# Attention denominators: ten blocks added by GpSimd, six by one DMA chain, two counted sums, reciprocals taken in place in PSUM

## The reference, cut to what matters

```
q = _heads(x @ Wq, B, L, nh, hd)                       # 16 heads of 32
decay_bias = -abs(pos[None, :] - pos[:, None]) * (1.0 - decay_factor)
out_short = _attention(q, k_s, v_s, decay_bias)        # softmax(q k^T / sqrt(hd) + bias) v
out_long  = _attention(q, k_l, v_l, None)
alpha = sigmoid(mix_weight)
out = alpha * out_short + (1.0 - alpha) * out_long     # then @ Wo
```

## Time and profile before

| | |
|---|---|
| median of 3 runs | 5075.12 us (5067.31 to 5075.18) |
| profiled execution | 5071.46 us |
| its span, first to last instruction | 5069.4 us |
| TensorE busy over the span | 4808.1 us (95%) |
| VectorE busy | 4044.8 us (80%) |
| GpSimd busy | 3012.3 us (59%) |
| ScalarE busy | 2998.2 us (59%) |

### The profile page before, as it was taken

The page is one execution under the profiler, slowest core; times in us unless marked ns, Lnnn a source line. Parts: engine busy times, 40 slices in busy tenths (PEclk is TensorE's granted clock), DMA queues, the critical chain, the costliest instruction groups (busy, mean ns, idle before and its releaser), DMA issues. The chain is left out here.

```text
span 5069.4 us, 101554 instructions
## 1 busy us (share of the span) xinstructions
PE 4808.1 (95%) x31276; PEld 2103.4 (41%) x31276; DVE 4044.8 (80%) x6613; ACT 2998.2 (59%) x5234; POOL 3012.3 (59%) x1267
## 2 busy tenths in 40 slices
PE   6888799999999999999999999999999599999998
PEld 3443233333333333333333333333332377777776
DVE  5556688888888888888888888888886388888887
ACT  2222166777676777777777777776767355555554
POOL 0000067878788888888887878888888233333332
PEclk9999789999999999999999999999999699999999
DMA  4332356777677776767676767777666200000000
GB/s 144 117 117 87 108 128 168 170 176 170 173 166 177 169 173 167 174 170 172 168 170 173 171 172 167 175 171 172 166 164 152 85 24 26 26 26 26 20 28 11
DMA packets 216978, 661.83 MB, mean 131 GB/s; under 512 B 38099, under 2 KB 111955, under 8 KB 158997
## 3 DMA queue, kind: packets, MB, share of 16 engines
q0 software_dynamic: 64512, 469.79, 39.8%
q1 hardware_dynamic: 151957, 185.66, 12.2%
HBM read 123.56 MB, written 61.64 MB: 37 GB/s over the span
## 5 line engine op out<-in xcount | busy, mean ns | idle before, releaser
L852 DVE TENSOR_REDUCE rowmax_parts<-scores_qk 128x1 f32<-128x512 f32 x4096 | 2524.6, 679 | 463.7 <-PE scores_qk L925 463.7
L832 ACT ACTIVATE probs_T<-scores_kq 128x512 f32<-128x512 f32 x4096 | 2286.3, 596 | 979.3 <-PE scores_kq L925 915.8
L766 POOL TENSOR_TENSOR probs_added<-probs_added,probs_T 128x2048 f32<-128x2048 f32 x448 | 2030.1, 4531 | 459.2 <-ACT probs_T L832 447.8
L925 PE MATMUL scores_kq<-q_operand,k_operand 103*128 103x512 f16 (+3 forms) x3712 | 1274.7, 349 | 10.2 <-ACT probs_T L832 8.3
L925 PE MATMUL scores_qk<-k_operand,q_operand 96*128 96x512 f16 (+4 forms) x3712 | 1123.1, 352 | 43.2 <-DMA k_operand<-positions_dram 19.4
L996 PE MATMUL outputs_T<-probs_T,v_operand 128*32 128x512 f32 x8192 | 1091.9, 605 | 1.3 <-ACT probs_T L832 1.3
L925 PEld LDWEIGHTS scores_kq<-q_operand,k_operand 103*128 103x128 f16 x3712 | 358.7, 97 | 920.9 <-ACT probs_T L832 635.7
L925 PEld LDWEIGHTS scores_qk<-k_operand,q_operand 96*128 96x128 f16 (+1 forms) x3712 | 354.8, 98 | 438.3 <-DVE rowmax_parts L852 184.4
L1602 PE MATMUL f_gate_up<-w_gate_up,xq_T 128*128 128x256 f16 (+1 forms) x4608 | 494.1, 265 | 8.6 <-DVE hidden L1493 7.5
L1602 PEld LDWEIGHTS f_gate_up<-w_gate_up,xq_T 128*128 128x128 f16 x4608 | 421.2, 98 | 77.8 <-issue 25.4
L766 POOL TENSOR_TENSOR probs_added<-probs_T 128x2048 f32<-128x2048 f32 x64 | 290.2, 4535 | 238.4 <-ACT probs_T L832 238.4
(11 more groups left out here) (165 smaller groups left out, 4302.1 us busy)
## 6 DMA issues: line engine op xcount, KB each, us to landing
probs_poured<-probs_T POOLq DMA_DIRECT2D x448, 1024.0 KB, 7.2
qk_parts_dram<-qk_parts SPq DMA_DIRECT2D x96, 256.0 KB, 2.5
q_operand<-qk_parts_dram SPq DMA_DIRECT2D x192, 128.0 KB, 2.6
k_operand<-qk_parts_dram SPq DMA_DIRECT2D x192, 128.0 KB, 3.1
v_dram<-v_heads SPq DMA_DIRECT2D x16, 1024.0 KB, 5.7
v_operand<-v_dram SPq DMA_DIRECT2D x64, 256.0 KB, 6.3
q_operand_above<-qk_parts_dram SPq DMA_DIRECT2D x96, 128.0 KB, 2.8
x_groups<-x SPq DMA_DIRECT2D x8, 1024.0 KB, 9.6
```

The source lines that it names most:

```text
L766: nc.gpsimd.tensor_tensor(total, first, probs[:, b % PBUF, :], ALU.add).then_inc(added.sem, 1)
L832: nc.scalar.activation(probs[:, kb % PBUF, qt * BANK:(qt + 1) * BANK], pb[:, k % 2, :], ACT.Exp)\
L852: nc.vector.reduce_max(rowmax[:, w % 2, c // NQ, c % NQ:c % NQ + 1], pa[:, k % 3, :], AX.X)\
L925: return nc.tensor.matmul(out, lhsT, rhs, start=start, stop=stop, skip_group_check=True)
```

## The change

The sixteen blocks of a unit are shared out anew. GpSimd adds ten (1, 2, 4, 5, 7, 8, 10, 11, 13, 14: nine add instructions where there were eight), and one DMA chain takes six (0, 3, 6, 9, 12, 15) in place of two chains with seven. The chain's tile is doubled, one for even and one for odd units. TensorE counts two tiles in place of three: GpSimd's in step 1 of the next unit and the chain's in step 4. ScalarE's copy of `sums` is gone: VectorE takes the reciprocals in place in PSUM, and `weigh`, now in step 9, reads them from there. The addition of the two kinds moves from VectorE to GpSimd's list, ahead of the add of block 11 in every second unit, and `weigh` of the next pair waits for it.

```diff
-WEIGH = 10
+WEIGH = 9
 MIX = 11
-BY_POOL = (0, 1, 3, 5, 7, 9, 11, 13, 14)
-BY_DMA = ((2, 6, 10), (4, 8, 12, 15))
+BY_DMA = (0, 3, 6, 9, 12, 15)
+BY_POOL = tuple(b for b in range(KB) if b not in BY_DMA)
-COUNT_POURED = (14, KB + 3)
 COUNT_ADDED = KB + 1
-TAKE_SUMS = 5
+COUNT_POURED = KB + 4
...
-            def pour(w, n, b, c):
+            def pour(w, n, b):
+                i = BY_DMA.index(b)
+                total, landed = poured_sum[:, w % 2, :], poured[w % 2]
                 wait_apart(pool, expd, expd.at(n, (w * KB + b + 1) * NQ), passed)
                 if i == 0:
+                    wait_apart(pool, counted_poured, counted_poured.at(n, w - 1), passed)
+                    nc.gpsimd.dma_start(total, probs[:, b % PBUF, :]).then_inc(landed.sem, 16)
                 else:
+                    wait_apart(pool, landed, landed.at(n, w // 2 * POURS + i), passed)
+                    nc.gpsimd.dma_start(total, probs[:, b % PBUF, :], accum_op=ALU.add).then_inc(landed.sem, 16)
+            def mix(p, n):
+                wait_apart(pool, weighed, weighed.at(n, 2 * p + 2), passed)
+                wait_apart(pool, stored[p], stored[p].before(n, NQ), passed)
+                nc.gpsimd.tensor_tensor(o_mix[:, p, :], o_w[:, 0, :], o_w[:, 1, :], ALU.add).then_inc(mixed.sem, 1)
...
-            def take_sums(w, n):
-                act.wait_ge(counted_poured[1].sem, counted_poured[1].at(n, w + 1))
-                act.wait_ge(weighed.sem, weighed.at(n, w))
-                nc.scalar.copy(sums[:, :], pc[:, :]).then_inc(sums_out.sem, 1)
...
             def invert(w, n, r):
-                dve.wait_ge(sums_out.sem, sums_out.at(n, w + 1))
-                nc.vector.reciprocal(inv[:, r * P:(r + 1) * P], sums[:, r * P:(r + 1) * P]).then_inc(inverted.sem, 1)
+                dve.wait_ge(counted_poured.sem, counted_poured.at(n, w + 1))
+                nc.vector.reciprocal(pc[:, r * P:(r + 1) * P], pc[:, r * P:(r + 1) * P]).then_inc(inverted.sem, 1)
...
-                nc.vector.scalar_tensor_tensor(o_w[:, w % 2, :], oT[:, w % 2, :], gates[:, 3 + w % 2:4 + w % 2], inv[:, :],
+                if w == 2:
+                    dve.wait_ge(mixed.sem, mixed.at(n, 1))
+                elif w == 0 and (not isinstance(n, int) or n > 0):
+                    dve.wait_ge(mixed.sem, mixed.before(n, 2))
+                nc.vector.scalar_tensor_tensor(o_w[:, w % 2, :], oT[:, w % 2, :], gates[:, 3 + w % 2:4 + w % 2], pc[:, :],
...
             def count_added(w, n):
+                pe.wait_ge(weighed.sem, weighed.at(n, w))
                 pe.wait_ge(added.sem, added.at(n, (w + 1) * ADDS))
-                count(added_sum[:, w % 2, :], counted, False, False)
+                count(added_sum[:, w % 2, :], counted, True, False)
+            def count_poured(w, n):
+                landed = poured[w % 2]
+                pe.wait_ge(landed.sem, landed.at(n, (w // 2 + 1) * POURS))
+                count(poured_sum[:, w % 2, :], counted_poured, False, True)
```

More of the change, by code:

```diff
@@ L574 @@
 INVERT = 5
-WEIGH = 10
+WEIGH = 9
 MIX = 11
-BY_POOL = (0, 1, 3, 5, 7, 9, 11, 13, 14)
-BY_DMA = ((2, 6, 10), (4, 8, 12, 15))
+BY_DMA = (0, 3, 6, 9, 12, 15)
+BY_POOL = tuple(b for b in range(KB) if b not in BY_DMA)
 ADDS = len(BY_POOL) - 1
-POURS = [len(blocks) for blocks in BY_DMA]
-COUNT_POURED = (14, KB + 3)
+POURS = len(BY_DMA)
 COUNT_ADDED = KB + 1
-TAKE_SUMS = 5
+COUNT_POURED = KB + 4
 def adds_until(kb):
@@ L619, in attend @@
         added_sum = sb("probs_added", [P, 2, L], F32)
-        poured_sum = [sb(f"probs_poured{i}", [P, L], F32) for i in range(2)]
+        poured_sum = sb("probs_poured", [P, 2, L], F32)
         rowmax = sb("rowmax_parts", [P, 2, KB, NQ], F32)
@@ L625, in attend @@
         oT = sb("o_T", [P, 2, BANK], F32)
-        sums = sb("sums_T", [P, BANK], F32)
-        inv = sb("sums_inverse", [P, BANK], F32)
         o_w = sb("o_weighed", [P, 2, BANK], F32)
@@ L652, in attend @@
         added = Rises(sem("a_added"), UNITS * ADDS, credit=1)
-        poured = [Rises(sem(f"a_poured{i}"), UNITS * POURS[i], 16) for i in range(2)]
+        poured = [Rises(sem(f"a_poured{i}"), UNITS // 2 * POURS, 16) for i in range(2)]
         counted = Rises(sem("a_counted"), UNITS, credit=1)
-        counted_poured = [Rises(sem(f"a_counted_poured{i}"), UNITS, credit=1) for i in range(2)]
+        counted_poured = Rises(sem("a_counted_poured"), UNITS, credit=1)
         taken = Rises(sem("a_o_taken"), UNITS, credit=1)
-        sums_out = Rises(sem("a_sums_out"), UNITS, credit=1)
         inverted = Rises(sem("a_inverted"), UNITS * NQ)
@@ L746, in _ @@
         def _(pool):
-            give_credit(pool, [maxed, expd, summed, added, counted, taken, sums_out, weighed] + counted_poured + stored)
+            give_credit(pool, [maxed, expd, summed, added, counted, taken, weighed, counted_poured] + stored)
             nc.gpsimd.memset(ones[:, :], 1.0).then_inc(consts, 1)
@@ L759, in add @@
                 wait_apart(pool, expd, expd.at(n, (w * KB + b + 1) * NQ), passed)
-                if b == 1:
-                    first = probs[:, 0, :]
+                if b == BY_POOL[1]:
+                    first = probs[:, BY_POOL[0], :]
                     wait_apart(pool, counted, counted.at(n, w - 1), passed)
@@ L766, in add @@
                 nc.gpsimd.tensor_tensor(total, first, probs[:, b % PBUF, :], ALU.add).then_inc(added.sem, 1)
-            def pour(w, n, b, c):
-                i = BY_DMA[c].index(b)
+            def pour(w, n, b):
+                i = BY_DMA.index(b)
+                total, landed = poured_sum[:, w % 2, :], poured[w % 2]
                 wait_apart(pool, expd, expd.at(n, (w * KB + b + 1) * NQ), passed)
                 if i == 0:
-                    wait_apart(pool, counted_poured[c], counted_poured[c].at(n, w), passed)
-                    nc.gpsimd.dma_start(poured_sum[c][:, :], probs[:, b % PBUF, :]).then_inc(poured[c].sem, 16)
-                else:
-                    wait_apart(pool, poured[c], poured[c].at(n, w * POURS[c] + i), passed)
-                    nc.gpsimd.dma_start(poured_sum[c][:, :], probs[:, b % PBUF, :], accum_op=ALU.add)\
-                        .then_inc(poured[c].sem, 16)
@@ L780, in one_pass @@
-            def one_pass(n):
-                for w in range(UNITS):
-                    for b in range(1, KB):
-                        if b in BY_POOL:
-                            add(w, n, b)
[L785 to L790, removed]
+                    wait_apart(pool, counted_poured, counted_poured.at(n, w - 1), passed)
@@ new lines, in one_pass @@
+            def one_pass(n, first, last):
+                for w in range(UNITS):
+                    back = unit_before(w, n, first)
+                    for b in range(KB):
+                        if b == MIX and back and back[0] % 2:
+                            mix(back[0] // 2, back[1])
+                        if b in BY_DMA:
+                            pour(w, n, b)
+                        elif b != BY_POOL[0]:
+                            add(w, n, b)
+            one_pass(0, True, False)
@@ L792, in _ @@
+            with nc.Fori(0, (PASSES - 2) // TURN, engines=[pool.engine], hint_back_edge=True) as m:
+                for i in range(TURN):
+                    one_pass(m * TURN + (i + 1), False, False)
+            one_pass(PASSES - 1, False, True)
+            mix(1, PASSES - 1)
         @block.scalar
@@ L812, in one_pass @@
                 for w in range(UNITS):
-                    back = unit_before(w, n, first)
                     for kb in range(KB):
-                        if back and kb == TAKE_SUMS:
-                            take_sums(*back)
                         if kb == (TURN_MAX + 2) % KB and after(w, n, last):
@@ L826, in one_pass @@
                         elif u >= 0 or not first:
-                            c = int(b in BY_DMA[1])
-                            act.wait_ge(poured[c].sem, poured[c].at(n, u * POURS[c] + BY_DMA[c].index(b) + 1))
+                            landed = poured[u % 2]
+                            act.wait_ge(landed.sem, landed.at(n, u // 2 * POURS + BY_DMA.index(b) + 1))
                         for qt in range(NQ):
@@ L839, in _ @@
             one_pass(PASSES - 1, False, True)
-            take_sums(UNITS - 1, PASSES - 1)
         @block.vector
@@ L904, in one_pass @@
                                 negate(*unit)
-                        if back and i == MIX and back[0] % 2:
-                            mix(back[0] // 2, back[1])
             one_pass(0, True, False)
@@ L912, in _ @@
             one_pass(PASSES - 1, False, True)
-            end = (UNITS - 1, PASSES - 1)
             for r in range(NQ):
-                invert(*end, r)
-            weigh(*end)
-            mix(1, PASSES - 1)
+                invert(UNITS - 1, PASSES - 1, r)
+            weigh(UNITS - 1, PASSES - 1)
         @block.tensor
@@ L1005, in count @@
                 mm.then_inc(done.sem, 1)
[L1007 to L1012, removed]
```

(9 more changed lines are left out.)

## The result

The changed kernel takes 5135.0 us (median of 4 runs, 5120.63 to 5141.65) against 5071.2 for the kernel before (5066.52 to 5075.18): a ratio of 1.0122, 95% interval 1.0098 to 1.0147. It is slower by about 62 us by that ratio (64 by the two medians), where 38 less had been forecast. The profiled execution took 5134.4 us, with a span of 5132.3.

What follows compares the result with a forecast made beforehand. The loop of exp, TensorE's product with v, count and next score was taken to set the pace; from 5071.5 us, -55 - 6 + 0 + 16 + 5 gave 5031.5, say 5033 us; range 5005 to 5110.

Steps and rivals of the forecast that it cites:

- Three counts become two: TensorE's counts in each unit: one count less saves 0.86 us in each of 64 units, -55.0 us.
- The weighing at step 9: `weigh` moved into VectorE's gap of 0.52 us: 0.1 us a unit, -6 us; bounds 0 and -20 us.
- Reciprocals in PSUM: VectorE's reciprocals written to PSUM: taken as 0; bounds -16 us and 40 us.
- Weighing beside GpSimd's adds: `weigh` on VectorE, reading one operand from PSUM, is not held while GpSimd adds: 0.
- GpSimd's list: GpSimd's work of 42.1 us, 0.1 for the semaphore and L turn in 50.7 us a unit: +16 us.
- L: Landing of block 0's pour, counted from its issue on GpSimd's queue: taken as 8.5 us, 11.2 beside loads.
- Some overlap is likely: Block 0's pour partly overlaps block 15's accumulating one, whose engines are not full all the time; L taken as 8.5.
- the undisturbed case: Block 0's data go behind the accumulating pour's, without loads beside: 6.9 + 2.7 - 0.9 = 8.7 us.
- the first rival: GpSimd becomes the bound: each us of L above 8.3 adds 63 us; slower, chance 0.20.
- its deciding point at 9.1: The L from which GpSimd's list turns in 51.3 us a unit and nothing is won.
- Other waits: Block 15's pour some 3 us later, its count one step later: just covered; exp's ring of eight blocks suffices.
- The end: Last unit: GpSimd falls 5 us further behind the last exp; the copy goes, the addition takes its time: +5 us.

Runs made afterwards that it cites:

- the first experiment: The kernel before with one count of its first DMA chain left out (blocks 2, 6 and 10 missing from the sums): 5016.7 us, ratio 0.9896.
- the second: The changed kernel with block 15's pour left out (the block missing from the sums): 5008.3 us, ratio 0.9876 to the kernel before.
- the last two experiments: Changed kernel with block 0's pour issued ahead of block 15's, plus the mixing back on VectorE: 5105.7 us; or plus reciprocals written to SBUF: 5360.9 us.
- the third experiment: The changed kernel with the loads of the next pass's operands issued six steps later: 5095.0 us, ratio 1.0043 to the kernel before.

## Why the prediction was wrong, point by point

- **Three counts become two**: right; 53 us measured, 55 said.
- **The weighing at step 9**: within its bounds. A unit with two counts takes 50.58 us with the weighing at step 10 (the first experiment) and 50.42 at step 9 (the second), 0.16 less; 0.1 had been taken. The two kernels differ in more than this step, so it is not a price of the step alone.
- **Reciprocals in PSUM**: nearly free, as taken. The row that answers to L874 of before has a median of 957 ns against 942:

```profile
L872 DVE RECIPROCAL sums<-sums x220: 953/957/960, 940.0 to 3779.3; 128x128 f32<-128x128 f32 x110
```

- **Weighing beside GpSimd's adds**: right. In the changed kernel `weigh` takes 734 to 742 ns, and the one of 2050.68 us ran beside an add that began at 2050.32 and took 4.53. The rule of the Trainium skill (GPSIMD Engine Reference, "1. Specifications"), that VectorE instructions with two SBUF inputs contend with GpSimd, is borne out by the last two experiments (2.7 and 4.15 us).
- **GpSimd's list**: well sized in the sum: 42.1 us and 0.1 for the semaphore said, 41.8 and 0.6 measured in the mean of 55 units. The semaphore's part was put too low by 0.5, the work too high by 0.3. A pour takes 0.91 us of the list (2013.76 to 2019.38, less an add of 4.71), 0.95 said; the moved addition 1.22 (2059.91 to 2061.13), 1.27 said.
- **"What is L? ... I take 8.5"**: this is the term that failed. L was 10.3 us in the middle. Behind long units it was 9.3 (8.0 to 11.2), behind short ones, which have ten loads beside them, 10.7 (8.7 to 11.9); the bound had been 11.2. Three choices made it too small. "Some overlap is likely": there was none. The sum for the undisturbed case started from the best landing of an accumulating pour, 6.9, and not from the middle one of 7.7, which gives 7.7 + 2.7 - 0.9 = 9.5; the third experiment measured 9.3. And the loads were thought partly done by then; moving them away took another 1.0 us off. With 10.3 in its own formula the prediction would have said 42.2 + 10.3 = 52.5 us a unit, 5071.5 + 63 x 1.1 + 5 = 5146; the run took 5134.4. So the mechanism was described, as the first rival, with its deciding point at 9.1; what was wrong is the size of L and, with it, the chance of 0.20 for that rival. The range ended at L = 9.7.
- The sentence of the Trainium skill that was weighed (DMA: Bandwidth & Descriptors, "Queues, rings and completion order") says ring order of the queues of SP and ScalarE; the windows at 2031 and 2084 agree with it for two pours on GpSimd's.
- **Other waits**: nearly right; TensorE waited 4.1 us in all for the chain at its count, in 10 waits. A link of the chain was at times late too (0.68 us at 2024.57). **The end**: the last exp ends at 4010.3 and the stores begin at 4031.6, 21.3 us later; before, 3941.1 and 3958.6, 17.5. 3.8 us more, 5 said.
- What the prediction did not have: TensorE's wait at the count lowers its clock now and then. At 1028 to 1030 us it was idle for 2.53 us, the clock fell to 0.51 until 1034, and the count took 1.94 us. This adds next to nothing to the loss: a later exp would have to reach GpSimd's list, and 95.3 of the 100.1 us that its adds wait for exp stand at the first add of a unit, which lies under the landing anyway (group view; busy us and mean ns, then idle before):

```profile
L762 POOL TENSOR_TENSOR probs_added<-probs_T 128x2048 f32<-128x2048 f32 x55 | 249.4, 4535 | 95.3 <-ACT probs_T L831 95.3
```

## What to carry to other kernels

When an engine's in-order list waits for a transfer that it issued itself, write down its whole circle (work, landing, restart) and price the landing in the place where the issue will stand, behind what is queued ahead of it, and not by its median elsewhere: two issues swapped were worth 113 us here. A saving on the pacing engine is only kept while the helpers that take over the work stay clearly under the new pace; here the helper's list had some 8.0 us (50.4 - 41.8 - 0.6) for a landing that took 10.3. And before work goes to GpSimd, look at which VectorE operations read two SBUF operands beside it.

## What the runs showed of the hardware that was not expected

- A plain copy of 1 MB issued 0.6 us behind an accumulating one of the same size on GpSimd's queue did not begin to move data until the other's were through, and landed after 8.0 to 11.9 us in place of 4.6.
- A VectorE operation with two SBUF operands that began beside a GpSimd add stood still until the add ended (4.05 us, ending 0.56 us after it, and 0.55 to 0.56 in all 80 cases), while one with an SBUF and a PSUM operand kept its 0.74 us.
- A TensorE stall of 3.31 us was followed by half clock until some 4 us after TensorE came back. A unit with one such stall was 5.65 us longer, though the weighing behind it was only 3.4 us longer; that the clock makes the difference is an estimate.
